# Token rows of four of eight expert places transposed by DMA instead of by TensorE

## What is computed

```python
h = layernorm(x)                       # 1024 tokens x 512
logits = h @ Wg + bg                   # 8 experts
one_hot = jax.nn.one_hot(jnp.argmax(logits, -1), 8)
y = gelu(h @ W1[e]) @ W2[e]            # for every expert e: 512 -> 2048 -> 512
x = x + y of the token's own expert
```

## Time and profile before

| what | value |
|---|---|
| median of 3 runs | 777.24 us (776.9 to 777.45) |
| the profiled execution, its own time | 777.18 us |
| its span, first to last instruction | 775.4 us |
| mean granted TensorE clock | 0.992 |
| PE busy | 754.9 us (97%) |
| DVE busy | 579.9 us (75%) |
| ACT busy | 472.4 us (61%) |
| POOL busy | 258.8 us (33%) |
| chain that ended last | PE 84%, DVE 10%, ACT 3% |
| DMA moved | 125.32 MB in 94854 packets |

### The profile page before, as it was taken

The page is one execution under the profiler, slowest core; times in us unless marked ns, Lnnn a source line. Parts: engine busy times, 40 slices in busy tenths (PEclk is TensorE's granted clock), DMA queues, the critical chain, the costliest instruction groups (busy, mean ns, idle before and its releaser), DMA issues.

```text
span 775.4 us, 21326 instructions
## 1 busy us (share of the span) xinstructions
PE 754.9 (97%) x8460; PEld 443.8 (57%) x8460; DVE 579.9 (75%) x1082; ACT 472.4 (61%) x848; POOL 258.8 (33%) x409
## 2 busy tenths in 40 slices
PE   8999999999999999999999999999798999999996
PEld 3455545555455544555445745466687688677773
DVE  5986767678676877666665677689789978888991
ACT  5556576657665676655765414425486786697871
POOL 0245334432454224432242110002332833163441
PEclk9999999999999999999999999999799999999999
DMA  9324553344233441445331621110769999889920
GB/s 329 136 66 114 143 137 90 84 112 112 43 86 95 112 107 37 113 107 139 57 99 29 174 103 54 55 55 7 266 243 386 415 414 393 332 339 392 383 77 30
DMA packets 94854, 125.32 MB, mean 162 GB/s; under 512 B 76368, under 2 KB 79184, under 8 KB 83908
## 3 DMA queue, kind: packets, MB, share of 16 engines
q1 hardware_dynamic: 91828, 116.64, 46.4%
q0 software_dynamic: 2384, 6.75, 2.4%
q10 hardware_dynamic: 576, 1.05, 0.4%
HBM read 100.24 MB, written 6.75 MB: 138 GB/s over the span
## 4 chain that ended last, share of the span: by engine, by line
PE 84%; DVE 10%; ACT 3%; issue 1%; POOL 1%; DMA 1%; POOLq 0%; DVEq 0%; ACTq 0%
PE bank L1624 63%; PE bank L2044 8%; PE bank L1793 4%; PE bank L1759 3%; DVE arena L990 3%; PE bank L2015 2%; ACT arena L710 2%; DVE arena L1005 1%; PE bank L1971 1%; PE bank L1662 1%; DVE arena L1027 1%; PE bank L1637 1%; DMA arena<-in_wk_t 1%; PE bank L1655 0%; ACT arena L944 0%
## 5 line engine op out<-in xcount | busy, mean ns | idle before, releaser
L1624 PE MATMUL bank<-arena 128*128 128x512 f16 (+11 forms) x3912 | 546.3, 300 | 5.7 <-DVE arena L1458 3.0
L1624 PEld LDWEIGHTS bank<-arena 128*128 128x128 f16 (+3 forms) x3912 | 308.7, 100 | 231.6 <-issue 7.1
L710 ACT ACTIVATE arena<-arena 128x256 f16<-128x256 f32 (+8 forms) x302 | 252.1, 883 | 18.7 <-DMA arena<-in_w 6.2
L990 DVE SCALAR_TENSOR_TENSOR arena<-arena 128x2048 f16<-128x2048 f32 (+4 forms) x101 | 200.3, 2006 | 24.0 <-ACT arena L710 23.9
L710 ACT ACTIVATE arena<-bank 128x512 f16<-128x512 f32 (+1 forms) x110 | 63.3, 591 | 102.3 <-PE bank L1624 69.8
L990 DVE SCALAR_TENSOR_TENSOR arena<-bank,arena 128x512 f16<-128x512 f32 (+1 forms) x109 | 73.2, 684 | 53.2 <-ACT arena L710 52.1
L2044 PE MATMUL bank<-arena 128*128 128x512 f16 x384 | 86.2, 379 | 0.0
L569 POOL TENSOR_TENSOR arena<-arena 32x1024 f16<-32x1024 f32 (+1 forms) x16 | 35.2, 2199 | 150.9 <-PE bank L1793 150.6
L717 ACT ACTIVATE arena<-bank,arena 128x512 f16<-128x512 f32 (+1 forms) x68 | 44.5, 664 | 59.4 <-PE bank L1624 55.8
L1017 DVE SCALAR_TENSOR_TENSOR arena<-bank,arena 128x512 f16<-128x512 f32 x64 | 47.5, 748 | 41.4 <-ACT arena L717 41.3
L748 ACT ACTIVATE arena<-arena 128x257 f32<-128x257 f32 x128 | 63.1, 498 | 0.0
(11 more groups left out here) (139 smaller groups left out, 523.2 us busy)
## 6 DMA issues: line engine op xcount, KB each, us to landing
arena<-in_w SPq DMA_DIRECT2D x64, 1024.0 KB, 8.0
arena<-in_ctx_t SPq DMA_DIRECT2D x15, 1024.0 KB, 5.4
arena<-in_awt SPq DMA_DIRECT2D x3, 1024.0 KB, 7.4
l_dram<-arena SPq DMA_DIRECT2D x4, 512.0 KB, 3.6
x_dram<-arena SPq DMA_DIRECT2D x1, 2048.0 KB, 8.7
arena<-in_ctx_t ACTq DMA_DIRECT2D x4, 256.0 KB, 5.4
arena<-in_wk_t SPq DMA_DIRECT2D x4, 256.0 KB, 6.0
arena<-in_wv_t SPq DMA_DIRECT2D x1, 1024.0 KB, 8.5
```

The lines of the kernel that those rows point to most:

```text
L710: return a.activation(dst, src, ACT.Copy, scale=scale)
L990: return v.scalar_tensor_tensor(dst, src, scale, h, ALU.mult, ALU.subtract)
L1624: last = m.matmul(out_ap, w, x, start=(n == 0), stop=(n == len(pairs) - 1))
```

## The change

A new constant names four places, 3, 4, 5 and 7. For these the PE transposes and VectorE's two copies are gone. In their place ScalarE, in `expert(n)` for the next place n + 1, waits until the rows have landed and issues one transposing transfer for each part, from `x_rows` straight to xs, on its own queue. This stands after the eight steps and ahead of piece 3 of the next place. TensorE waits for their landing (`xs_landed`) at the start of a turned place. GpSimd waits for it, where it waited for the transposes of that place, before it gathers the rows of the next. Places 1, 2 and 6 stay as they were, with counters that count only them. ScalarE gets one `sem_inc` more after its wait.

```diff
+TURNED = (3, 4, 5, 7)
...
+        def by_dma(n):
+            return isinstance(n, int) and n in TURNED
+        def turned_by_pe(n):
+            return sum(not by_dma(e) for e in range(1, n + 1)) if isinstance(n, int) else n - len(TURNED)
+        def turned_by_dma(n):
+            return 16 * sum(PARTS[e] for e in TURNED if e <= n)
...
 # GpSimd, expert(n, e)
-                    pool.wait_ge(s["xt_ps"], n)
+                    if by_dma(n):
+                        pool.wait_ge(s["xs_landed"], turned_by_dma(n))
+                    else:
+                        pool.wait_ge(s["xt_ps"], turned_by_pe(n))
                     pool.sem_inc(s["pool_waits"], 1)
                     gather_tokens(n + 1, e + 1)
...
 # ScalarE
+            def token_rows(n):
+                act.wait_ge(s["x_rows_landed"], rows_before(n + 1) - 16 * PARTS[0])
+                act.sem_inc(s["act_waits"], 1)
+                by_chunk = xs.rearrange("p z c x -> p (z c) x")
+                for part, (lo_, hi_) in enumerate(((0, P), (P, CAP))[:parts_of(n)]):
+                    act.dma_start_transpose(by_chunk[:, :, lo_:hi_], x_rows[part]).then_inc(s["xs_landed"], 16)
...
                 if nxt:
+                    if by_dma(n + 1):
+                        token_rows(n + 1)
                     piece_hi(n + 1, 3)
...
 # VectorE
-                dve.wait_ge(s["xt_ps"], n)
+                dve.wait_ge(s["xt_ps"], turned_by_pe(n))
...
                 if nxt:
-                    gathered(n + 1)
+                    if not by_dma(n + 1):
+                        gathered(n + 1)
...
 # TensorE, expert(n)
-                pe.wait_ge(s["xs_done"], n * 2 + 2)
+                if by_dma(n):
+                    pe.wait_ge(s["xs_landed"], turned_by_dma(n))
+                else:
+                    pe.wait_ge(s["xs_done"], turned_by_pe(n) * 2 + 2)
...
-                    if nxt and c == (1 if first else 0):
+                    if nxt and c == (1 if first else 0) and not by_dma(n + 1):
                         token_transposes(n + 1)
```

More of the change, by code:

```diff
@@ L331, in perceiver_block @@
         products unbound even_ps even_added irfft_ps x2_done chain_dve chain_pool pool_waits
-        gate_landed l2_shift l2_normal x2_stored l2_stored x_rows_landed own_done xt_ps ids_taken ids_sorted ids_ps wg_split gate_spectra_ready gate_tokens_ps l2_hi l2_lo lt_ps lt_done logits_ps onehot_done rank_ps count_ps routed
+        gate_landed l2_shift l2_normal x2_stored l2_stored x_rows_landed own_done xt_ps xs_landed act_waits ids_taken ids_sorted ids_ps wg_split gate_spectra_ready gate_tokens_ps l2_hi l2_lo lt_ps lt_done logits_ps onehot_done rank_ps count_ps routed
         e_landed0 e_landed1 e_landed2 e_landed3 e_landed4 e_landed5 e_landed6 e_landed7 e_hi e_lo perm_done first_ps xs_done h_ps gelu_done h_hi h_lo
```

## The result

| | before | after |
|---|---|---|
| median | 777.35 us (4 runs) | 791.44 us (786.46 to 798.79, 4 runs) |
| ratio, 95% interval | | 1.0165 (1.0147 to 1.0183) |
| span of the profiled execution | 775.4 us | 789.5 us |
| PE busy, mean granted clock | 754.9 us, 0.992 | 757.0 us, 0.98 |
| longest landing of a transfer of token rows | | 24.1 us |

The changed kernel is 1.65% slower. The forecast was 0.31% faster. (The slowest of its four runs, 798.79 us, counts as a slow one and is in the median but not in the ratio.) What happened is the event of the second rival, rows that land late, at one place only.

What follows compares the result with a forecast made beforehand. PE, busy for 97% of the span, was taken as the bound; -2.38 us of transposes with nothing given back gave 777.24 - 2.4 = 774.8 us, forecast range 774.2 to 775.6, reaching to 788 with late landing.

Steps and rivals of the forecast that it cites:

- the second rival: Starts of places 3, 4 and 5: rows land late behind weight packets, PE waits 11, 7, 8 us; 787 us, chance 0.30.
- PE's transposes, -2.38 us: Places 3, 4, 5 and 7: transposes leave PE's chain, 0.74, 0.74, 0.45 and 0.45 us.
- DVE, DMA load, GpSimd: Turned places: DVE's saved copies counted as nothing, 1.8 or 1.4 us more DMA work and later gathers cost nothing.
- starts 21.8 us after place 5 as before: Start of place 6: moves with place 5's start, the 1.0 us stall stays, and the earlier gain is kept.
- ACT's issues: ScalarE's transposing issues before piece 3: 1.6 us for places 3 and 4, 1.1 us for 5 and 7, costing PE zero.
- the room at place 3: Time from ACT's issue to place 3's start, less the removed transposes: 9.3 us, issue beginning at 637.7.
- The landing, 7.0 us for two parts: Turned places: transfer lands 7.0 us after issue, 6.5 us for one part, fitting with 1.5 to 2.3 us spare.
- 3.4 us of crowding: Added to the 3.6 us landing alone, from token gathers beside weights: 4.1 us at best, 7.5 median.

Runs made afterwards that it cites:

- The version with one queue: Changed kernel with the transposing transfers of places 3, 4, 5 and 7 issued from SP's queue between its weight loads; 774.58 us, ratio 0.9976.
- the run without place 3: Changed kernel with place 3 back on TensorE, so only places 4, 5 and 7 turned by DMA; 775.48 us, ratio 0.9981.
- the second execution: The changed kernel run once more, nothing altered, for a second trace; 797.39 us.
- the run with weights held: Changed kernel with SP issuing no further weight load until the transposing transfers landed, at every turned place; 780.18 us, ratio 1.0045.
- the run held at place 3 only: Changed kernel with SP issuing no further weight load until place 3's transfers landed, nothing held for places 4, 5 and 7; 794.77 us, ratio 1.0233.
- the six-place version: Transposing transfers from SP's queue for places 2 to 7, against the same from SP for places 3, 4, 5 and 7; 776.64 us, ratio 1.0006.
- the run with small packets: Changed kernel with each 1 MB weight load split into four by columns, packets 2 KB instead of 8 KB; 785.15 us, ratio 1.0112.

## Why the prediction was wrong

**PE's transposes, -2.38 us: right.** 0.73, 0.45 and 0.46 us by the stretches above. The version with one queue reached 774.58 us where the sum said 774.8, but that near is partly luck: its stretches gain 1.90 us, and the ratio allows 0.8 to 3.0 us.

**DVE, DMA load, GpSimd: right or harmless.** PE ran on without a gap into places 4, 5 and 7.

**Place 6, "starts 21.8 us after place 5 as before": wrong, a smaller miss.** The 1.0 us stall released by DVE's copies was gone, but PE stood still inside place 5 instead. The place took 22.94 us in the changed kernel, 22.59 in the run without place 3, and 22.52 with one queue. So 0.7 to 1.1 us of the 2.38 us are lost again, to a term that the sum did not have.

**ACT's issues: mis-sized, without effect.** 1.34 us for the first part (1.1 forecast), but 1.3 to 2.65 us for the 32-row part, for which I had taken 0.45 us from a plain transfer. They held ACT's sequencer for 2.5 to 4 us at a two-part place, and its room took it in. They also began earlier than forecast, at 634.3 for place 3 where 637.7 less this execution's lead of 1.3 us is 636.4. The prediction had the issue wait until piece 2 is done; in the second execution it begins at 635.61 and piece 2 at 635.90. So the room at place 3 was 11.5 us and not 9.3.

**The landing, 7.0 us for two parts: the step that failed.** It was 23.0 to 24.1 us at place 3, and 28.0 to 29.8 us in the second execution. At place 4 it was 4.1 us, below the 7.0, at places 5 and 7 6.2 and 7.2 us for a forecast 6.5. The prediction said that the nearest rows were the token gathers, with 3.4 us of crowding. They carry the same bytes, but the engines take turns by packets and not by bytes. In the trace before, the gathers of place 4's 160 rows are 80 packets of 4 KB, 5 for each engine, where the transposing transfers are 1280 packets, 80 for each engine. The size of the latter stood in the earlier trace rows. The second rival had those turns and their price (80 turns of 0.32 us, 26 us). It got 0.30 by comparison with a transfer of another packet size. That comparison should not have counted.

**The second rival in detail.** Its turns are real: rows and weight packets alternate one for one (150 against 160, 738 against 739). Its 11 us for place 3 came near the 14.1 us by luck. It let the stall end when the weight queue ran dry, and took turns at full pace until then. Neither was so: weight loads issued during the transfer still landed up to 672.9, 13 us after PE had gone on, and most of the rows were through before PE came. Its 8 us and 7 us for places 5 and 4 did not come. Those transfers met a gap in the weight queue, which SP's rhythm leaves there: a load goes out only when VectorE frees a buffer. I had read that the engines are 92% busy there and not asked when the other 8% are. Its clock term was missing: 2.85 us.

**What alternation does not explain.** In the profiled execution of the changed kernel the queues between 644 and 654, inside the wait, and the weights issued in 641 to 645:

```profile
DMA packets 387, 1.15 MB, mean 115 GB/s; under 512 B 255, under 2 KB 255, under 8 KB 255
...
q1 hardware_dynamic: 145, 1.07, 80.9%
q10 hardware_dynamic: 241, 0.06, 29.3%
...
L467 SPq DMA_DIRECT2D arena<-in_w x2: 333/333/333, 642.7 to 644.8; - x2
...
DMA to landing us min/median/max: 22.9/23.6/24.4
```

Pure alternation would keep the weights at about 400 GB/s, as it did in 692.5 to 695.5 of the run with weights held. Here both together moved 115 GB/s, and weights that otherwise land in 9 us took 23. So 23 to 24 us lies near 80 turns of 0.3 us, but turns at full pace are not the account of it: the two kinds of transfer also hold each other up. The traces have it where new weight loads came in while a transfer was half done (place 3 here and in the second execution, place 4 of the run held at place 3 only) and not where they were held, though not every time that they came in: place 5's transfer of the changed kernel was under way from 704.0 to 710.2, a load was issued at 707.2, and nothing was held up. The trace does not tell which engine carried a packet. How the engines block each other is not settled by these runs.

## What to carry to other kernels

Ask of a transfer on a second queue how many packets it has on each DMA engine and how large the other queue's packets are. Turns go one for one, so 80 small rows beside 8 KB packets that never let up would take 80 x 0.3 us, whatever their bytes; in these runs the damage also came with the engines mostly idle. Put it into the queue that carries the bulk, where it waits for the backlog once, or into a moment at which that queue is empty. Such an empty moment can be lost by any shift of the schedule, as the hold at place 3 showed at place 4. Hold the bulk loads back only with care: with a hold at every turned place the kernel took 780.18 us, more than before.

## What I had not expected of the hardware

A transposing transfer of 32 rows holds ScalarE's sequencer as long as one of 128 rows or longer: 1.26 to 1.34 us for the first part, 1.29 to 2.65 us for the second, up to 4.99 us with weights around. From SP's queue between weight loads the issues took 1.8 to 4.6 us, in the six-place version up to 9.4 us. I read this as an issue that also waits while its queue is backed up; no run tests it.

The wait of 14.1 us cost TensorE another 2.85 us afterwards: the granted clock went from 1.00 (2.4 GHz) to 0.50 (1.2 GHz) while it idled, was still 0.50 in the first 4 us of matmuls, 0.78 in the next 4 and 1.00 from 668 on. The price does not grow with the wait. It was 1.70 us after 19.78 us (15.15 for 13.45), 1.26 us after 17.99 us (12.79 for 11.53) and 1.51 us after only 2.83 us (11.12 for 9.61), and nothing after 2.81 us in the run with small packets (13.46).
